# Matmuls whose result is not read, behind each gather of the weight dequantisation on TensorE

## What is computed

```python
wq = qw[:, None, :] >> shifts[None, :, None] & NIB
return sc[g_idx] * (wq - zq[g_idx])                     # _dequant
...
x = x + _L0_xattn_ref(_layernorm(x), ctx_4096, ctx_4096, Wq, bq, Wk, bk, Wv, bv, interference, amp, Wo, bo)
...
inter = jnp.einsum('bsh,hf->bsf', x, w_gu)              # 512 -> 2 x 1376
gate, up = (inter[..., :INTER], inter[..., INTER:])
h = jax.nn.silu(gate) * up
x = x + jnp.einsum('bsf,fh->bsh', h, w_d)               # 1376 -> 512
```

## Time and profile before

| | |
|---|---|
| median of 3 runs | 880.54 us (879.96 to 883.99) |
| the profiled execution, its own time | 883.46 us |
| its span, first to last instruction | 881.7 us |
| mean granted clock of TensorE | 0.938 |
| TensorE busy | 798.8 us, 91% |
| VectorE, ScalarE, GpSimd busy | 487.5, 427.4, 296.9 us |
| matmuls | 10119 |

### The profile page before, as it was taken

One profiled execution on the slowest core, in us unless ns is written; L12 is line 12 of the kernel. 1 busy time (PEld: TensorE's weight loads), 2 busy tenths in 40 slices (PEclk: granted clock), 3 DMA queues, 4 the chain that ended last, 5 costly groups with the idle time before them and its releaser, 6 DMA issues.

```text
span 881.7 us, 24230 instructions
## 1 busy us (share of the span) xinstructions
PE 798.8 (91%) x10119; PEld 569.5 (65%) x10119; DVE 487.5 (55%) x1000; ACT 427.4 (48%) x817; POOL 296.9 (34%) x297
## 2 busy tenths in 40 slices
PE   5465778899999999999999999999999999999898
PEld 5411324565787578757875787578757876787484
DVE  9878563453656465646564656465646564644421
ACT  1656566353665166516651665166516652565020
POOL 2155355243144304430443044304430443054020
PEclk9755666999999999999999999999999999999899
DMA  8943122000100110011001100110011000100000
GB/s 281 261 107 93 52 72 84 26 3 1 52 2 4 50 52 2 3 50 52 2 3 50 52 3 3 50 51 3 3 50 49 5 3 25 28 2 15 13 1 25
DMA packets 21509, 37.09 MB, mean 42 GB/s; under 512 B 4158, under 2 KB 8414, under 8 KB 21404
## 3 DMA queue, kind: packets, MB, share of 16 engines
q1 hardware_dynamic: 21404, 35.48, 13.7%
HBM read 26.47 MB, written 4.19 MB: 35 GB/s over the span
## 4 chain that ended last, share of the span: by engine, by line
PE 69%; DVE 10%; issue 8%; ACT 7%; SPq 2%; DMA 1%; POOL 1%; DVEq 0%; ACTq 0%; POOLq 0%
PE bank L556 17%; PE bank L571 13%; PE bank L527 10%; PE bank L537 9%; PE bank L696 4%; PE bank L713 3%; DVE nmf L1274 3%; PE bank L583 3%; PE bank L690 3%; ACT arena L917 3%; PE bank L504 2%; PE bank L671 2%; DVE arena L1206 1%; DVE stats L1211 1%; SPq L377 1%
## 5 line engine op out<-in xcount | busy, mean ns | idle before, releaser
L556 PE MATMUL bank<-arena,WGU 128*128 128x256 f16 (+1 forms) x2112 | 248.2, 274 | 1.4 <-DVE arena L761 1.4
L556 PEld LDWEIGHTS bank<-arena,WGU 128*128 128x128 f16 (+1 forms) x2112 | 206.9, 101 | 27.9 <-DVE arena L761 1.6
L1462 POOL TENSOR_TENSOR arena<-arena 128x512 f16<-128x512 f32 x128 | 146.8, 1173 | 209.5 <-ACT arena L924 209.5
L571 PE MATMUL bank<-WD,arena 128*128 128x512 f16 (+1 forms) x528 | 121.0, 379 | 0.0
L917 ACT ACTIVATE arena<-bank,small 128x512 f32<-128x512 f32 x128 | 89.1, 775 | 58.6 <-PE bank L696 58.6
L1452 POOL TENSOR_TENSOR arena<-arena 128x512 f16<-128x512 f32 (+1 forms) x48 | 51.6, 1076 | 181.3 <-ACT arena L900 181.3
L527 PE MATMUL bank<-arena,WT 128*128 128x256 f16 x768 | 90.5, 280 | 11.6 <-issue 9.1
L527 PEld LDWEIGHTS bank<-arena,WT 128*128 128x128 f16 x768 | 76.8, 100 | 25.4 <-issue 14.3
L537 PE MATMUL bank<-WT,arena 128*128 128x512 f16 x384 | 87.2, 384 | 0.0
L571 PEld LDWEIGHTS bank<-WD,arena 128*128 128x128 f16 (+1 forms) x528 | 49.4, 97 | 53.2
L1274 DVE TENSOR_REDUCE nmf<-bank 128x8 f32<-128x512 f32 x128 | 79.3, 681 | 5.5 <-PE bank L671 5.3
(11 more groups left out here) (172 smaller groups left out, 1049.2 us busy)
## 6 DMA issues: line engine op xcount, KB each, us to landing
arena<-in_L_ffn_qweight_gu SPq DMA_DIRECT2D x8, 688.0 KB, 5.4
arena<-arena SPq DMA_DIRECT2D x32, 144.0 KB, 2.6
WT<-in_ctx SPq DMA_DIRECT2D x8, 512.0 KB, 10.0
arena<-in_ctx SPq DMA_DIRECT2D x8, 512.0 KB, 4.0
arena<-in_x SPq DMA_DIRECT2D x8, 512.0 KB, 3.5
out_y<-arena SPq DMA_DIRECT2D x16, 256.0 KB, 2.1
arena<-in_L_ffn_qweight_down SPq DMA_DIRECT2D x10, 256.0 KB, 3.5
arena<-in_L_xattn_Wk SPq DMA_DIRECT2D x1, 1024.0 KB, 5.5
```

Source lines behind the costliest of these rows:

```text
L556: mm = e.matmul(pb[0:m, i * TOK:(i + 1) * TOK], WGU[:, sp, kb, half * INTER + fb * P:half * INTER + fb * P + m], x2T[:, mp, kb, :], start= ...
L571: mm = e.matmul(pb[:, :], hT[0:m, sp, fb, t * P:(t + 1) * P], WD[0:m, mp, fb, :], start=(n == 0), stop=(n == 3 * FB - 1))
L1462: e.tensor_tensor(phl[:, a, 1, :], pring[:, a, :], phl[:, a, 0, :], ALU.subtract).then_inc(S["p_lo"], 1)
```

## The change

Behind the gather of each tick from the third on TensorE issues three more matmuls of 512 columns. Their weights are 96 rows of a 16-bit identity, their moving operand 96 rows of the one-hot matrix, both ready since the first gather. They write to an attention bank that is free at that time, `AB[0]`, or `AB[2]` at "keys", where banks 0 and 1 hold the key projection. Each overwrites the one before, and nothing reads them. In "values", where `AB[0]` has held keys, the place begins with a wait for the second eviction of the keys. Ticks 37 to 39 have no gather any more (there are 35 units), but have their three matmuls.

```diff
         def pe_ticks(e, place):
+            idle = AB[2] if place == "keys" else AB[0]
+            if place == "values":
+                e.wait_ge(S["qk_evicted"], 2)
             for n in ticks(place):
                 pe_dequant(e, n - 2)
+                for _ in range(3 if n >= 2 else 0):
+                    e.matmul(idle[:, :], ident16[0:96, :], hot_gu[0:96, :], start=True, stop=True)
```

## The result

The changed kernel takes **901.9 us** (median; 901.04 to 903.38) where the kernel before takes 880.83: a ratio of **1.0244**, 95% interval 1.0216 to 1.0273. The profiled execution took 901.99 us, its span 900.3, 18.6 more than the span before.

The account below looks back on a forecast made before the run. TensorE was taken as busy at full clock from 154 us, so only the preparation before it counted: 1.2 - 1.4 - 1.5 + 0 + 0.4 + 1.2 - 1.7 = -1.8 us, giving 878.7 us, range 875 to 888.

Parts of the forecast that it names:

- How long it stays low: Gather bursts of the preparation: the clock rises after 4.7 us of dense work, the middle of 3.0 to 6.4.
- Rival 1: Preparation: narrow matmuls never raise the clock in the bursts, nothing is won back; +31 us, 912 us; chance 15%.
- Price at half clock, +0.88 a tick: Gather ticks while the clock is low: 2.62 us with the fillers against 1.74, TensorE then the bound.
- Fillers 0.43 and 0.216 us apart: Spacing of the added matmuls at half and full clock; three cost 1.28 or 0.65 us.
- rival 2: Gather ticks: each filler waits for its own weight load, warm ticks gain nothing; +6.7 us, 887 us; chance 10%.
- -0.28 a tick at full clock: Gather ticks once the clock is high: faster gathers save 0.28 us each; TensorE itself needs about 1.44.
- Twelve fillers: Behind the fifth burst's last gather: 2.6 us of fillers push the eight transposes, which then go at double speed; +1.2 us.
- Rival 3: Pauses before bursts four and five: shortened by 0.65 us, the clock outlasts them; 4.2 us less, 874.5 us; chance 15%.
- The nothing in the eight chunks: Chunks after the preparation: the change adds no instruction there, so a gain beyond 160 us would have no place.
- nine tenths or more from slice 7 on: Reading of the earlier profile: from slice 7 (154 us) TensorE is that busy, with its clock at full speed.

Follow-up runs that it names:

- the version with the lowest median: Kernel before plus 128-row fillers in the pauses behind gathers 10, 18, 28 and two in most later ticks, 8-column matmuls up to 114 in all: 872.93 us, 0.9897.

## Why the prediction was wrong

**The forecast, 878.7 us within 875 to 888, failed at the step "How long it stays low".** It took 4.7 us from two rises in streams of 128-row matmuls (a third, at 121.24, came 5.0 us after TensorE's last pause) and used it for bursts in which a third of the matmuls are 4 or 68 rows deep and half are 96. There was no rise in any burst. Rival 1 named that mechanism, with 15%; it is what happened, and the range left it out. The experiment with 128 rows shows that even where the clock rises, it takes 5.5 to 10.2 us, and the first scores come 5.3 us later, not 1.8 earlier.

By its own terms:
- *Price at half clock, +0.88 a tick*: right. In the third burst six ticks took 15.86 us (82.67 to 98.53), 2.64 for the 2.62 of the text, against 1.74.
- *Fillers 0.43 and 0.216 us apart*: right, 1.28 us for three, 0.65 with 128 rows at full clock. So rival 2 didn't happen. The Trainium skill's rule, which stands in "TensorE: Matmul & The Clock Gate", section "The mechanism", and not in the section that the prediction names, is that a weight load runs beside matmuls only in another row group. It doesn't hold for these fillers, which all use the same rows.
- *-0.28 a tick at full clock*: not seen in the change. With 128 rows a wide tick took 1.51 us where I had 1.50 as TensorE's own need.
- *Rival 1's sum, +31*: the mechanism was right, the sum 6 too high at the scores. The third burst with its trailing fillers cost 6.7 us (rival: 6.6), the fourth 8.3 (7.9), the fifth with the twelve 9.9 (rival: 9.9). The difference lies where it said "nothing is won back": 3.0 us for the second burst and not 4.4; 1.9 us in the pauses before gathers 19 (0.6) and 29 (1.3), which took up some of the delay; and 3.1 between the transposes and the scores, as the twelve raised the clock.
- *Twelve fillers*: +1.2 expected, at full clock. They ran at half clock for 4.98 us; leaving them out gives 2 to 3 us.
- *Rival 3*: refuted. The clock fell in each pause, at 111.64 and 149.18 too, although the pauses had shrunk to 3.83 and 2.39 us (2.0 and 2.3 us into them).
- *"The nothing in the eight chunks"*: wrong, and not among the rivals. The 114 matmuls with their weight loads moved the loop's start, which gave back 6.9 us after the scores: standstills of 0.8 us in place of 9.1, so 8.3, less 1.6 of a clock that fell in the first chunk. The rows for it (five standstills of 1.8 us in the chain) were in the trace of the kernel before, and I didn't read the chain beyond the preparation. Without this gain the change would have cost some 28 us (21.1 and 6.9); with 67 more matmuls of no work it cost 39.7.
- *A reading*: "nine tenths or more from slice 7 on" isn't what the earlier trace rows say. Slice 7 itself and a few near the end stand at eight; nothing in the sum hangs on it.

Two errors of opposite sign, then. Ahead of the scores the forecast said 1.8 us earlier and they came 25.5 later, which makes 27 us; behind them it said nothing and 6.9 us were won.

## What to carry to other kernels

Count on fillers to raise TensorE's clock only in a mixture that has been seen to raise it: here three of 96 rows between gathers of 68, 4 and 128 rows never did, three of 128 rows did, and 96 rows in a row did. A filler at half clock is paid at twice its price until then, so put fillers where the clock is up already, or in pauses. Any edit that adds or removes instructions ahead of a loop can change each pass; compare the time of a pass and the idle time at its start before the gain or loss is put down to the edit, and use as many instructions without work as the control.

## What the runs showed of the hardware

- TensorE without a pause for 22 us (82.67 to 104.82) at a granted clock of 0.50; the same program with 128-row fillers rose after 5.5 to 10.2 us.
- The clock rose 4.9 us into twelve 96-row matmuls in a row and 3.5 us into fifteen; within twelve 32-row ones, 5.2 us, it didn't.
- With the change the clock fell 1.0 us behind a pause of 2.25 us in the first chunk, and behind the same pause before it didn't; in the version with the lowest median it fell 0.6 us behind a pause of 1.84 us.
- A jump back in TensorE's program cost from 0.1 to 3.3 us, by the count of instructions ahead of the loop: 1.8 to 1.9 at each jump with none added, 2.2 to 3.3 (behind the first 8 matmuls) with 53 and with 181 matmuls added, and with 102, 114 and 128 either 0.1 to 0.3 or 1.7 to 2.1 from jump to jump. What decides between jumps is open.
- The fetches of instructions stand in the trace, in packets of 16.4 KB: two at once, of 1.5 to 2.2 us, ahead of each standstill of 1.7 to 2.1 us, and one, of 0.9 to 1.1 us, ahead of the jumps without.
- At half clock a 32-row matmul starts 0.54 us behind a 128-row one of 512 columns, and a 96-row one 0.40.
